# A fourth tile of attention features, with queries, projection and squares rearranged

## The reference

```
mod = (silu(c) @ wmod)                      # six vectors of 128 for each batch
h = layernorm(x) * (1 + ca) + sa
q, k, v = split(h @ qkv_w.T + qkv_b)        # 16 heads of 8; rotary on q and k
p = softmax(causal(q k^T / sqrt(8)))
x = x + ga * ((p v) @ proj_w.T + proj_b)
h = layernorm(x) * (1 + cb) + sb
y = square(relu(h @ W_fc.T)) @ W_proj.T     # 128 -> 512 -> 128
x = x + gb * spikes(y)                      # five threshold tests, counted, / 5
```

## Time and profile before

| | |
|---|---|
| median of 3 runs | 441.04 us (440.73 to 445.44) |
| profiled execution, its own time | 443.15 us |
| profiled execution, its span | 441.4 us |
| mean granted clock | 0.988 |
| PE, DVE, ACT, POOL busy | 89%, 75%, 58%, 29% |
| transfers | 38.53 MB, mean 87 GB/s |

### The profile page before, as it was taken

The page is one execution under the profiler, slowest core; times in us unless marked ns, Lnnn a source line. Parts: engine busy times, 40 slices in busy tenths (PEclk is TensorE's granted clock), DMA queues, the critical chain, the costliest instruction groups (busy, mean ns, idle before and its releaser), DMA issues.

```text
span 441.4 us, 15622 instructions
## 1 busy us (share of the span) xinstructions
PE 390.9 (89%) x6599; PEld 253.1 (57%) x6599; DVE 329.3 (75%) x730; ACT 256.8 (58%) x447; POOL 126.1 (29%) x163
## 2 busy tenths in 40 slices
PE   2778899888999989998899999998998889988885
PEld 2327555555656755666457654765566646753653
DVE  6659995886886988878986997699866777541176
ACT  8203465565676756765666665766665457566523
POOL 6714310430343043503342234304330220040020
PEclk9989999999999999999999999999999899998999
DMA  7056363243314233242415251323233050011001
GB/s 214 22 161 169 99 218 88 70 116 102 104 45 119 75 101 93 80 122 49 137 50 139 64 138 48 117 72 99 67 113 86 16 146 6 25 45 27 3 1 49
DMA packets 26050, 38.53 MB, mean 87 GB/s; under 512 B 5796, under 2 KB 20716, under 8 KB 23692
## 3 DMA queue, kind: packets, MB, share of 16 engines
q1 hardware_dynamic: 25980, 37.53, 29.8%
HBM read 26.35 MB, written 8.65 MB: 79 GB/s over the span
## 4 chain that ended last, share of the span: by engine, by line
PE 41%; DMA 18%; DVE 13%; ACT 10%; POOL 6%; issue 5%; SPq 5%; ACTq 0%; POOLq 0%; DVEq 0%
PE o_bank L611 10%; DMA kf<-k_scr 9%; PE d_bank L528 7%; DVE negmax L978 6%; PE t_bank L593 6%; PE s_bank L548 5%; DMA rden<-r_scr 4%; ACT probs L827 4%; PE a_bank L528 3%; DMA r_scr<-rden_c 2%; POOL parts L1303 2%; PE s_bank L528 2%; SPq L440 2%; PE t_bank L528 2%; POOL o_n L1325 2%
## 5 line engine op out<-in xcount | busy, mean ns | idle before, releaser
L978 DVE TENSOR_REDUCE negmax<-s_bank 128x1 f32<-128x512 f32 (+7 forms) x368 | 192.9, 566 | 56.9 <-PE s_bank L554 54.6
L827 ACT ACTIVATE probs<-t_bank 128x512 f32<-128x512 f32 x288 | 163.0, 594 | 89.8 <-PE t_bank L598 84.5
L548 PE MATMUL s_bank<-kf,qf 126*64 126x512 bf16 (+7 forms) x1024 | 118.7, 293 | 11.8 <-DMA kf<-k_scr 6.2
L593 PE MATMUL t_bank<-qf,kf 128*64 128x512 bf16 (+7 forms) x1024 | 113.3, 290 | 10.8 <-ACT probs L827 9.8
L611 PE MATMUL o_bank<-probs,v 128*32 128x512 f32 (+7 forms) x1024 | 75.1, 412 | 0.0
L548 PEld LDWEIGHTS s_bank<-kf,qf 126*64 126x64 bf16 x1024 | 50.6, 111 | 40.6 <-DVE negmax L978 19.9
L554 PE MATMUL s_bank<-causal,identb 128*64 128x64 bf16 x1024 | 72.6, 195 | 0.0
L598 PE MATMUL t_bank<-causal_t,identb 128*64 128x64 bf16 x1024 | 64.8, 195 | 0.0
L593 PEld LDWEIGHTS t_bank<-qf,kf 128*64 128x64 bf16 x1024 | 41.4, 110 | 35.1 <-ACT probs L827 14.4
L598 PEld LDWEIGHTS t_bank<-causal_t,identb 128*64 128x64 bf16 x1024 | 48.1, 111 | 9.3 <-issue 0.2
L554 PEld LDWEIGHTS s_bank<-causal,identb 128*64 128x64 bf16 x1024 | 47.1, 112 | 8.3 <-issue 8.1
(11 more groups left out here) (145 smaller groups left out, 455.9 us busy)
## 6 DMA issues: line engine op xcount, KB each, us to landing
qf<-q_scr SPq DMA_DIRECT2D x15, 576.0 KB
kf<-k_scr SPq DMA_DIRECT2D x45, 192.0 KB
q_scr<-parts SPq DMA_DIRECT2D x24, 128.0 KB, 1.7
k_scr<-parts SPq DMA_DIRECT2D x24, 128.0 KB, 1.7
xa<-in_x SPq DMA_DIRECT2D x8, 256.0 KB, 3.9
o_t<-o_raw SPq DMA_DIRECT2D x60, 32.0 KB, 2.4
rden<-r_scr SPq DMA_DIRECT2D x15, 128.0 KB
out_y<-count SPq DMA_DIRECT2D x7, 256.0 KB, 6.7
```

The costliest lines, as they stand in the source:

```text
L548: nc.tensor.matmul(bank[C * a:C * (a + 1), col:col + keys], qf[0:KS, slot, 2 * p + a, C * i:C * (i + 1)], kf[0:KS, slot, 2 * p + a, 0:keys ...
L593: nc.tensor.matmul(bank[C * a:C * (a + 1), col:col + w], kf[0:KX, slot, 2 * p + a, C * kb:C * (kb + 1)], qf[0:KX, slot, 2 * p + a, C * kb: ...
L827: nc.scalar.activation(probs[:, v, :], t_bank[u % 2][:, :], ACT.Exp, scale=SCALE).then_inc(e_done, 1)
L978: last = nc.vector.tensor_reduce(own[:, i, p:p + len(same)], cols, AX.X, ALU.max, negate=True)
```

## The change

`RING` becomes 4: half n uses tile n % 4, and queries wait for half n - 4. To make room, the remainder of the split (`rest`) lies in rot_s, the squares lie in place of relu, the modulation weights in part of relu, and the row of ones in part of count. ACT clears the fourth tile in the setup, behind the first values.

On SP the queries of half 2b+4 are issued at the end of iteration b, behind the second part of the keys and so ahead of the third; the keys follow behind the third as before. Numbers and sizes of the transfers for a half stay as they are; the one transfer of ones goes to four tiles in place of three.

PROJ goes from slot 16 to 17 and residual 1 from 18 to 19 in all but the last batch; the reciprocals of the second half go from slot 10 to 9. The second and third rotary steps wait for the end of the previous split in place of the previous sum.

```
-RING = 3
+RING = 4
...
-D_AT = {16: PROJ, 25: T2, 27: FC, 29: FC + 1, 31: FC + 2, 33: FC + 3}
+D_AT = {17: PROJ, 25: T2, 27: FC, 29: FC + 1, 31: FC + 2, 33: FC + 3}
...
-        wmod_sb = sb("wmod_sb", [P, 6 * P])
-        ones_row = sb("ones_row", [MR, SEQ], BF16)
...
-        rest = sb("rest", [P, 2, SEQ])
+        rest = rot_s
...
-        sq = sb("sq", [P, NF, SEQ])
+        sq = relu
+        wmod_sb = relu[:, 0:2, :].rearrange("p i c -> p (i c)")[:, 0:6 * P]
         count = sb("count", [P, 2, SEQ])
+        ones_row = count[0:MR, 0, 0:SEQ // 2].bitcast(BF16)
...
             sp.wait_ge(ones_made, 1)
-            sp.wait_ge(zeros_made[2], 2)
+            for slot in (2, 3):
+                sp.wait_ge(zeros_made[slot], 2)
...
                 if 0 < b < final:
                     store_part(b + 1, 1, 2)
-                if 0 < b < final:
-                    spread(2 * b + 2)
+                    spread_keys(2 * b + 2)
...
                 if b + 2 < NB:
                     store_part(b + 2, 1, 1)
+                    spread_queries(2 * b + 4)
...
             place_values(0)
+            clear(3, qf)
+            clear(3, kf)
             modulate1(1)
...
-                reach(dve, whole_done, 2 * (b - 1) + qk + 1)
+                reach(dve, whole_done if step == 0 else split_done, 2 * (b - 1) + qk + 1)
...
-                    if at == (8 if b == final else 10):
+                    if at == (8 if b == final else 9):
                         reciprocals(b - 1, 1)
-                    if at == 18:
+                    if at == (18 if b == final else 19):
                         residual1(b - 1)
```

## The result

The changed kernel takes 446.16 us (median of four, 445.51 to 446.29) against 440.88 us: ratio 1.0146, 95% interval 1.0104 to 1.0188. It is slower, just outside the range of 429 to 446, and not the 438.4 that was forecast. The profiled execution took 445.51 us with a span of 443.8, against 443.15 and 441.4. So the two profiles show 2.4 us of a loss of 5.3; the profile of before caught an execution 2.3 us above its median.

A forecast was written before the change was run, and what follows sets the result against it. TensorE, busy 89% of the span, was taken as the bound, its stalls counting once. Terms -3.3 + 5.6 - 3.2 - 1.7 = -2.6 us, off the median of 441.04, gave 438.4 us; range 429 to 446.

The forecast's parts named there:

- part 2: Even halves on SP, queries ahead of the keys' third part: keys land at T+12.9, stalls 8.5 us from 2.9, +5.6 us.
- I take T+6.0: Even halves: the keys' third part lands 6.0 us after T, the moment SP has issued the keys' second part.
- part 4: PE's clock and the rest: one half-clock stretch after two stalls over 1.3 us goes, -1.7 us, 0 as other end.
- Part 1: Odd halves on SP: the fourth tile ends the wait for the tile's release, so their key stalls go, -3.3 us.
- The slower rival: Even halves: third part takes 8.0 us, keys land at T+14.9, 448 us; decides from T+13.3; chance 0.15.
- drained data: Setup transfers: data behind the queries had drained by 51 us, 6 us after the queries were issued.
- the setup's landing: Setup transfers: 8.0 us from queries to the third part's landing, taken as a high end for the store.
- The low end of T+2.65: Even halves: the keys' third part lands at T+2.65, as if the queries ahead held nothing.
- Part 3: Projection a slot later, reciprocals a slot earlier: output waits -5.7 us, VectorE +2.5 us, together -3.2 us.
- The 2.5 us for VectorE: Reciprocals in the earlier slot wait for sums ahead of VectorE's maxima: 0.5 us in five batches.
- The rest at nothing: Two more ACT clears, larger ones transfer, squares, borrowed tiles and the rotary steps' new wait: no cost expected.

The follow-up runs named there:

- third_by_pool: Changed kernel, but the keys' third part of batches 2 to 7 is stored by GpSimd's own queue, queries still ahead: 442.26 us, ratio 1.0042.
- slots_back: Changed kernel with projection in slot 16, residual 1 in slot 18 and reciprocals in slot 10 again: 445.62 us, ratio 1.0117.
- half4_third_first: Changed kernel with the old order, queries behind the keys' third part, for half 4 alone: 439.0 us, ratio 0.9996.
- borrowed_alone: Kernel before, three tiles, with only the shared tiles and the rotary steps' new wait: 440.52 us, ratio 1.0018.
- order_alone: Kernel before, three tiles and old slots, with only the even queries ahead of the keys' third part: 448.28 us, ratio 1.0181.
- half_queries_ahead: Changed kernel with even queries split, 288 KB ahead of the keys' third part and 288 KB behind it: 436.48 us, ratio 0.9898.
- pool_store_unhurried: The control: changed kernel, GpSimd's queue stores the keys' third part and SP issues even queries only once it has landed: 446.29 us, ratio 1.0116.

## Why the prediction was wrong

The step that failed is in part 2: "I take T+6.0" for the third part's landing, where the changed kernel shows T+6.6 on average. With it part 2 came out at +5.6 us and measured +9.8. The sign of part 4, the clock, was wrong as well.

*Part 1, odd halves, -3.3 us*: right. No odd half stalls after the change.

*Part 2, even halves, +5.6 us*: the mechanism was right, and this is the term that was mis-sized; it turned the sign. PE wanted the keys where I said (T+11.8 to T+12.1 in five halves, T+9.8 in half 4). But they landed at T+12.8 to T+14.6, 13.6 on average, where the sum had T+12.9. Of the 0.7 us of difference 0.6 are in the step "I take T+6.0" (6.6 on average, 5.9 to 7.1) and the rest in the keys' 6.9 us (7.0). Small each, but paid six times, as the sum could have said: 12.7 us of stall against 8.5, +9.8 in place of +5.6. The slower rival named T+13.3 as the point from which it decides, and 13.6 is past it; its own T+14.9 and 448 us were an over-statement. I had given it 0.15. The 6.6 lies between the 6.0 of the drained data and the 8.0 of the setup's landing, nearer the 6.0, and the setup's own figure is not firm: the same place takes 6.7 to 8.3 us in the profiles of the other runs. The 6.0 had been read off where little data flowed any more, and not off a landing. The low end of T+2.65 was half 10's; half 4 had T+4.3 already before the change (96.46 against 92.15), with the queries behind the store.

The Trainium skill's page "DMA: Bandwidth & Descriptors", section "Queues, rings and completion order", says more than I took from it: the increment waits for earlier writes of its DMA engine "across its queues". The time in third_by_pool agrees (4.8 against 2.5 us), but bytes that are themselves late would show the same. The Trainium skill's fixed cost of about 2 us (the same page, "Anatomy of one DMA") is given there for transfers that GpSimd issues, and the prediction applied it to SP's store. Of GpSimd's stores the control's median of 2.5 us is near it, and the 4.8 us with the queries under way are not.

*Part 3, -5.7 + 2.5 us*: the stalls for outputs went to nothing, as said. The 2.5 us for VectorE were 0.4 us in this kernel: PE waits for maxima 2.4 us against 2.0, though the reciprocals wait 17.9 us for the sums, and slots_back shows most of that turn into waiting for scores. The mechanism is real all the same: in half4_third_first, with shorter key stalls, it costs the 2.4 us that were estimated. What a VectorE wait costs is to be read from whether PE stands at the same time.

*Part 4, the clock, -1.7 us*: wrong in sign. The half-clock stretch after the projection went, but one of 6.8 us came with the longer stall of half 4 and one of 3.4 us behind half 8's, and the loop's loss at half clock went from 3.1 to 4.0 us. I had priced only one of two stretches before and none after, though I expected a stall of 3 us in half 4.

*The rest at nothing*: right for what the change moves: borrowed_alone measures 1.0018, and ACT's two clears fit ahead of modulate 1, which still comes after 2.9 us idle. The 1.2 us for the maxima's rows at 61.92 I did not foresee; it stands in this profile and, smaller, in some others with the old order (0.66 us in borrowed_alone), so it is not put down to the change.

*The miss in numbers*: 446.16 us against 438.4 is 7.8 us. Of these 5.0 are between the profiles (+2.4 where the sum had -2.6): keys +4.2, clock +2.6, outputs and VectorE -2.1, small waits +0.5, together 5.2. The other 2.8 us are scatter between profiled executions and medians. I took the gain off the median, but read it in a profile that ran 2.3 us above it. That the 1.7 us at half clock are in a median execution at all was never shown: borrowed_alone, with the old order, was profiled at 440.75 us with no such stretch in its loop.

## What to carry to other kernels

Keep large transfers from starting ahead of a small one that others wait for. Here 576 KB ahead turned a store of mostly 1.7 us into one of 4.9 to 6.0 us in SP's queue, and one of 2.5 us into one of 4.8 us in GpSimd's, and the large transfer gained only 1.3 us of start for it. When a wait is late in every iteration, multiply a half microsecond of doubt by its count before trusting the sign of the sum: this step was put at 6.0 us, and the sign of the sum turned at 6.4. And a change that bundles a good part with a bad one is worth taking apart: the fourth tile and the slots without the new order give 433.15 us, 1.7% under the kernel before.

## What the hardware showed that I had not expected

In the loop, all eight stalls of TensorE of 2.58 us and more came with a stretch at half clock, 1.2 GHz, that began during the stall or up to 1 us behind it: 4.92 us in the changed kernel (6.8 us at 0.50), 4.76 in order_alone (6.8), 4.09 and 2.58 in slots_back (3.4 and 6.8), 3.17 in half_queries_ahead (6.8), 2.66 in third_by_pool (3.4), 3.44 and 3.95 in pool_store_unhurried (3.4 and 6.8). None of the five between 2.0 and 2.5 us did (2.00 in the changed kernel, 2.05, 2.19, 2.44 and 2.49 in other runs). Of those between 1 and 2 us some did: 1.53 us in the kernel before, 1.83 in the changed one, while half4_third_first went through six of 1.08 to 1.78 us at full clock. And the stretch at 399.9 us in the kernel before follows no stall over 0.6 us in the 8 us ahead of it. So the longest stalls here carried this second price each time, but the length of one stall does not tell whether it is paid.
